# First attention: the raw value copy behind the turned copies on ACT, the key remainder ahead of the value remainder on POOL

## What is computed

```
xq = rope(x @ Wq)        # (b, s, 32, 16)
xk = rope(x @ Wk)        # (b, s, 8, 16), each head used by 4 query heads
xv = x @ Wv              # (b, s, 8, 16)
scores = einsum("bqhd,bkhd->bhqk", xq, xk) / 4, masked causally
out = softmax(scores) @ xv, heads joined, @ Wo
x = layernorm(x + out)
```

## Time and profile before

| | us |
|---|---|
| median of 3 runs | 802.99 |
| lowest and highest | 796.69, 803.73 |
| the profiled execution | 801.41 |
| its span (first to last instruction) | 799.6 |

### The profile page before, as it was taken

How to read it: one execution, slowest core, us unless ns; L and a number is a source line. 1 busy time by engine, 2 the same in 40 slices (tenths; PEclk the granted TensorE clock), 3 DMA queues, 4 the chain that set the end, 5 groups by cost and what they waited for, 6 DMA issues and landing times.

```text
span 799.6 us, 13805 instructions
## 1 busy us (share of the span) xinstructions
PE 762.1 (95%) x4809; PEld 650.7 (81%) x4809; DVE 597.0 (75%) x1143; ACT 322.8 (40%) x684; POOL 403.7 (50%) x381
## 2 busy tenths in 40 slices
PE   6799999989999999999999999999999999999996
PEld 4687777779878888888888888888888888888875
DVE  4678888977877677677767767776776767688777
ACT  4555555563333333342333334233333423234335
POOL 7566666674644554453455445345544534544303
PEclk9799999999999999999999999999999999999999
DMA  8710004012252223322322332222233223141002
GB/s 183 193 33 18 16 16 121 5 56 55 66 146 80 54 63 74 103 52 52 79 52 63 73 101 52 52 79 52 65 72 100 53 54 79 28 105 27 2 0 106
DMA packets 107876, 53.56 MB, mean 67 GB/s; under 512 B 80448, under 2 KB 96960, under 8 KB 107840
## 3 DMA queue, kind: packets, MB, share of 16 engines
q1 hardware_dynamic: 107008, 51.51, 25.6%
q10 hardware_dynamic: 576, 1.05, 0.4%
q0 software_dynamic: 256, 0.52, 0.3%
HBM read 32.62 MB, written 2.10 MB: 43 GB/s over the span
## 4 chain that ended last, share of the span: by engine, by line
PE 65%; DVE 14%; POOL 9%; issue 6%; ACT 3%; DMA 2%; SPq 1%; DVEq 0%; POOLq 0%; ACTq 0%
PE bank L767 18%; PE bank L702 15%; PE bank L506 10%; PE s_bank L781 4%; DVE arena_r L1693 3%; PE s_bank L783 2%; PE bank L530 2%; POOL arena_f L1453 2%; PE bank L751 2%; PE bank L927 2%; DVE small L1789 2%; POOL arena_r L1476 2%; ACT arena_r L1036 1%; PE s_bank L751 1%; DVE arena_f L1777 1%
## 5 line engine op out<-in xcount | busy, mean ns | idle before, releaser
L767 PE MATMUL bank<-arena_r 128*128 128x512 f32 x768 | 191.5, 398 | 0.0
L702 PE MATMUL bank<-arena_r 128*128 128x512 f32 x720 | 185.1, 400 | 2.2 <-POOL arena_r L1534 1.7
L1036 ACT ACTIVATE arena_r<-bank 128x256 fp32r<-128x256 f32 (+2 forms) x249 | 104.8, 460 | 201.2 <-PE bank L734 84.4
L767 PEld LDWEIGHTS bank<-arena_r 128*128 128x128 f32 x768 | 139.6, 188 | 27.0
L702 PEld LDWEIGHTS bank<-arena_r 128*128 128x128 f32 x720 | 130.6, 188 | 31.5 <-POOL arena_r L1534 2.1
L506 PE MATMUL bank<-arena_r 128*128 128x256 f32 (+1 forms) x1056 | 147.5, 295 | 1.2 <-issue 0.6
L506 PEld LDWEIGHTS bank<-arena_r 128*128 128x128 f32 x1056 | 137.6, 192 | 9.1 <-DVE arena_r L1693 2.3
L1693 DVE TENSOR_TENSOR arena_r<-bank,arena_r 128x256 fp32r<-128x256 f32 (+2 forms) x217 | 99.5, 485 | 43.3 <-ACT arena_r L1036 42.4
L1036 ACT ACTIVATE arena_r<-arena_f 128x512 fp32r<-128x512 f32 (+1 forms) x178 | 103.9, 638 | 59.9 <-DMA arena_f<-arena_f 44.6
L1693 DVE TENSOR_TENSOR arena_r<-arena_f,arena_r 128x512 fp32r<-128x512 f32 (+1 forms) x95 | 88.9, 944 | 15.9 <-ACT arena_r L1036 15.6
L1525 POOL TENSOR_TENSOR arena_f<-arena_f 128x512 f32<-128x512 f32 x30 | 39.2, 1305 | 114.3 <-DVE arena_f L1882 114.2
(11 more groups left out here) (164 smaller groups left out, 1205.7 us busy)
## 6 DMA issues: line engine op xcount, KB each, us to landing
arena_f<-arena_f SPq DMA_DIRECT2D x120, 128.0 KB, 2.5
arena_f<-in_L_xattn_Wo SPq DMA_DIRECT2D x8, 1024.0 KB, 5.9
arena_f<-in_L_xattn_Wq SPq DMA_DIRECT2D x14, 512.0 KB, 4.0
arena_f<-in_x SPq DMA_DIRECT2D x8, 256.0 KB, 2.9
arena_f<-in_x SPq DMA_DIRECT2D x1, 2048.0 KB, 10.4
arena_f<-in_L_xattn_Wk SPq DMA_DIRECT2D x8, 256.0 KB, 3.1
arena_f<-in_L_xattn_Wv SPq DMA_DIRECT2D x8, 256.0 KB, 3.4
arena_f<-in_ctx SPq DMA_DIRECT2D x8, 256.0 KB, 3.1
```

Source lines behind the costliest of these rows:

```text
L702: mm = pe.matmul(BQ2[f][:], w2q_s[a][:, e, j, f, :], xT[b][:, e, tok], start=(e == 0 and n == 0), stop=(e == EC - 1 and n == 2))
L767: mm = pe.matmul(BO2[i][:], at2[a][:, h, i * P:(i + 1) * P], w2o_s[b][:, h, :], start=(h == 0 and n == 0), stop=(h == HG - 1 and n == 2))
L1036: act.activation(dst, src, ACT.Copy).then_inc(done, 1)
```

## The change

Two lines move. On ACT `value_raw(i + 1)` goes from between the high copies of the third and fourth block to behind `turned_copies(i + 1)`. On POOL `key_low(i + 1)` goes ahead of `value_low(i)`. Both are in the branch of the step for i = 0 to 6.

```diff
@@ ACT, tile_steps
                 p_high(i, 2, not old)
-                value_raw(i + 1)
                 p_high(i, 3, not old)
                 if not ahead:
                     wq_high(0, 0)
                     wq_high(0, 1)
                 turned_copies(i + 1)
+                value_raw(i + 1)
@@ POOL, tile_steps
                 norm(i, 3)
+                key_low(i + 1)
                 value_low(i)
-                key_low(i + 1)
```

## The result

| | before | after |
|---|---|---|
| median of 16 runs, us | 801.63 (the three shown ahead are among them) | 793.33 |
| profiled execution, us | 801.41 | 796.18 |
| span, mean granted clock | 799.6, 0.987 | 794.4, 0.984 |

The changed kernel takes 0.9915 of the time before (95% interval 0.9894 to 0.9936), 6.8 us less by that ratio; the two medians of the table lie 8.3 us apart. One of the 16 runs before took 1890.24 us and stands outside the ratio, which compares fast runs alone. Two later comparisons of the same two kernels gave 0.9926 (0.9898 to 0.9954) and 0.9910 (0.9874 to 0.9946). So it is faster, by 6 to 7 us.

The account below looks back on a forecast made before the run. TensorE, busy 95% of the span, was held by a closed chain of waits in each first-attention tile. 0.55 + 5 x 0.95 + 1.0 = 6.3 us gave 795.1 or 796.7, by base; forecast 796.0, range 791.5 to 800.5.

Parts of the forecast that it names:

- The stall and its cause: First attention's tiles: ACT's fourth high copy waits only by queue order behind the raw value copy; moving it wins 0.95 us a tile.
- The raw copy costs nothing: ACT, behind the last turned copy: the 0.28 us raw value copy hides in ACT's 3.65 us wait for POOL's subtraction.
- SP's queue: Value transfers and the load of x issue later; 4.2 us of room, 1.2 in the last tile; cost nothing, bounds 0 and 1 us.
- The key remainder beside the query remainder: POOL's key remainder, slowed beside DVE's query remainder, takes 2.15 us and ends 0.1 us before DVE; bounds 1.27 and 1.27 + 1.02.
- Tile 0: First tile's step, where TensorE's granted clock is 0.50 from 42 to 45 us: gain 0.55 us, bounds 0.47 and 0.95.
- Tile 6: Step with two weight copies between high copy and turned copies, chain on ACT: all four copies come about 1.0 us earlier.
- The sum: Whole kernel: 0.55 for tile 0, 5 x 0.95 for the steady tiles, 1.0 for tile 6, together 6.3 us.
- Rival 1: Key turn: POOL's key remainder ends last, so the gain is smaller; half-way case 4.5 us, 797.7 us; chance 0.08.
- Rival 2: Behind tile 7, staging the first head group: a transfer bounds it and the gain is lost; 801 to 803 us; chance 0.07.
- Rival 3: POOL's key remainder issues first and shuts out DVE's query remainder: 2.3 us slower, 804.5; chance 0.05 together with a late x load.
- Rival 4: Whole kernel: more than 8 us won; nothing in the trace gives it, only the scatter of the runs; no separate chance.

Follow-up runs that it names:

- the swap alone: Only POOL's key remainder moved ahead of the value remainder, raw value copy left in its old place, against the kernel before: ratio 1.0224, and 1.0232 when run again.

## Why the prediction was right

Forecast: 796.0 us, 0.8% down (6.3 us), range 791.5 to 800.5, "within 1%" at 0.70. Measured: 793.33 us, ratio 0.9915, so 0.85% down.

- **The stall and its cause.** Right. The fourth high copy stood behind the raw copy for its place alone, and its 0.95 us a tile came out as 0.96 in each of tiles 1 to 3 (the table: 3.17 - 2.21, 4.13 - 3.17, 5.09 - 4.13), and as 1.90 over tiles 4 and 5.
- **The raw copy costs nothing.** Right, 0.31 us inside a wait of 3.49. Halfway along the queue it cost all that the change wins.
- **SP's queue.** Right in that nobody waits. The load's lead is 6.8 us; the tightest place, the value copy in tile 7, still runs at its place, at 163.97, 8.05 us earlier than in the earlier trace rows, like its neighbours.
- **The key remainder beside the query remainder.** Forecast 2.15 us, ending 0.1 us ahead of DVE; measured 2.27 and 0.08. The full stop named as the upper bound was 2.29. It lost 1.00 us of an overlap of 1.13 (96.13 to 97.26); the overlap is longer than in the earlier trace rows, where the value remainder started 0.22 us behind DVE, since the key remainder starts only 0.13 behind. By the rule of the Trainium skill (SBUF — State Buffer, section Who interferes with whom) the one that issues second is shut out until the first is done. With this trace's rows that makes an estimate of 97.26 + 1.27 = 98.53 for the end; 98.40 was measured, so the trace agrees but for 0.13 us. That it works both ways, the first to come holding the other up, no row of before showed; the kernel with the early query remainder did (1.84 instead of 1.26 us on DVE).
- **Tile 0.** The term was mis-sized: 0.55 forecast, 1.48 in the two profiles. I charged it with half speed because one profile showed 0.50 there. In the changed kernel's profile the same stretch stood at 1.00, and its own repetitions differ by 2.4 us in this step. The bounds (0.47 to 0.95) were those of one execution's clock, not of the kernel.
- **Tile 6.** 1.0 forecast, 1.07 measured (8.06 - 6.99).
- **The sum** was 6.3; up to tile 7 it came out at 7.33 in the two profiles, nearly all of the difference in tile 0, and at the end some 3 us went again for which the sum had no term. The three ratios make 5.9 to 7.2 us of the whole kernel, so the total is right, but in part by luck: tile 0 was put too low for this pair of profiles, and the loss at the end was not seen. What the runs confirm is the sum's main term, 5 x 0.95. The forecast time was 2.7 us too high: the base, the mean of 801.41 and 802.99, stands 0.6 us above the median of 16, and the rest, 2 us, lies inside the runs' scatter.
- **Rival 1** (the key remainder last) did not come true, by 0.08 us. **Rival 2** (given back later) did not come true where it was looked for: 8.06 us in tile 7 are 8.03 at the start of the second attention's subtractions. But 3.2 of 8.40 us were given back at the end of the second attention, by the clock and not by a transfer. **Rival 3** (DVE shut out): the order of starts held (96.00 before 96.13); in the kernel of the early query remainder, where a POOL instruction came first, DVE was held up. **Rival 4** (more than 8 us won): the pair of profiles shows 8.06 in tile 7, but 0.73 of it was there before the change acts, and about 0.9 above the forecast is tile 0's scatter.

What the prediction did not see is what the clock can do. Behind the stop of 1.0 us ahead of the key turn it never fell in tiles 2 to 6. Behind a stop of 2.2 us at the same place it fell in four tiles of six, and such a tile took up to 24.3 us instead of 21.2. Had the change made the wait longer instead of shorter, my sum would have been off by half, as it was for the swap alone. And the clock fell in the second attention, which the change does not touch.

## What to carry to other kernels

An instruction that waits for a slow neighbour holds up everything behind it in its in-order queue: look in the chain of waits for a step whose only link to the next is the queue, and put it behind the last thing that the bounding engine waits for, not merely one place further. Ask of the two gates of a wait how far they lie apart, since a freed gate is worth only the distance to the other (here 0.41 of 0.96 us a tile until POOL's order was changed too). When an order makes TensorE stand still longer, count the clock as well as the gap; where such a gap can't be avoided, idle turns in it can win something back (here half of the loss). Compare the profiles to the very end of the kernel too: a gain that is won early can be given back by the clock in a part that nobody changed.

## What the runs showed of the hardware

- TensorE's granted clock: with a stop of 1.0 us in each tile it stays at 1.00 over tiles 2 to 6; behind stops of 2.2 us at the same place it falls to its lower level for some 7 us in four of six tiles, and 16 idle turns (1.91 us) in that stop keep it at 1.00. The idle turns were plain turns of the identity. The length of the stop alone does not decide: the same stop of 1.2 us late in the second attention is followed by 0.50 in all three profiles of the changed kernel and by 1.00 in the kernel before.
- The mean granted clock of an execution goes along with much of the runs' scatter: 789 us at 0.996, 796 at 0.983, for one kernel.
- In these runs a POOL instruction with SBUF inputs and a DVE one with two SBUF inputs held each other up, whichever came first: POOL lost 1.00 us of an overlap of 1.13, DVE 0.58 of 0.77. The losers lost 0.13 and 0.19 us less than the rows overlap.
